# Rotating the last block's keys on GpSimd behind the second and third blocks' keys

## The reference

```python
x = x + mamba(layernorm(x))                      # in_proj, conv of 4 taps, selective scan over 16 states, out_proj
x = x + cross_attention(layernorm(x), ctx, pos, mask)
x = x + mixture(layernorm(x))                    # 64 experts of rank 8, the best 16 by a router

# cross attention: 32 heads of q, 8 heads of k and v (each serves 4 heads of q), head size 128
q = rows(query @ Wq);  k = rows(ctx @ Wk);  v = rows(ctx @ Wv)
cos, sin = tables[position_ids]
q = q * cos + rotate_half(q) * sin
k = k * cos + rotate_half(k) * sin               # rotate_half swaps the halves of the 128 and negates one
scores = q @ k.T / sqrt(128), masked with -1e9;  softmax;  @ v;  @ Wo
```

## Time and profile before

| | us |
|---|---|
| median of 3 runs | 2348.61 |
| lowest and highest | 2341.81, 2349.77 |
| the profiled execution's own time | 2350.73 |
| its span | 2349.1 |
| TensorE busy | 2086.0 (89%) |
| VectorE busy | 1762.5 (75%) |
| ScalarE busy | 1003.9 (43%) |
| GpSimd busy | 701.3 (30%) |
| seam behind stage 1, behind stage 2 | about 890 to 1000, about 1430 to 1540 |
| last stage | from about 2010 |

### The profile page before, as it was taken

How to read it: one execution, slowest core, us unless ns; L and a number is a source line. 1 busy time by engine, 2 the same in 40 slices (tenths; PEclk the granted TensorE clock), 3 DMA queues, 4 the chain that set the end, 5 groups by cost and what they waited for, 6 DMA issues and landing times.

```text
span 2349.1 us, 26708 instructions
## 1 busy us (share of the span) xinstructions
PE 2086.0 (89%) x8268; PEld 1192.0 (51%) x8272; DVE 1762.5 (75%) x1735; ACT 1003.9 (43%) x2549; POOL 701.3 (30%) x492
## 2 busy tenths in 40 slices
PE   6877887898999988998999989998999989799988
PEld 2333454345555543445556544345556544477774
DVE  4499994459999996259999996259999994456553
ACT  2544440265555532155545541255545540233331
POOL 0289992401111112401111111501111110456550
PEclk9788999889999999989999999989999999799999
DMA  2579895527888873435888874525887874332210
GB/s 63 165 178 230 210 215 169 146 95 175 176 182 196 184 180 101 154 117 135 186 190 179 186 166 119 186 91 136 190 190 181 188 166 117 103 99 90 86 59 18
DMA packets 117810, 352.12 MB, mean 150 GB/s; under 512 B 14016, under 2 KB 14144, under 8 KB 115296
## 3 DMA queue, kind: packets, MB, share of 16 engines
q0 software_dynamic: 40704, 146.82, 32.3%
q1 hardware_dynamic: 70112, 191.68, 26.6%
q10 hardware_dynamic: 6912, 12.59, 1.4%
HBM read 197.68 MB, written 23.33 MB: 94 GB/s over the span
## 4 chain that ended last, share of the span: by engine, by line
DVE 34%; PE 27%; DMA 17%; issue 14%; ACT 3%; POOL 2%; DVEq 1%; PEldq 1%; SPq 0%; POOLq 0%; PEld 0%; ACTq 0%
DMA xc<-hs 15%; DVE hs L1254 11%; DVE hs L1431 4%; PE acc L1753 4%; PE acc L1631 3%; DVE hs L1261 3%; DVE hs L1245 2%; PE pq L1684 2%; PE acc L1837 2%; PE pq L1714 2%; PE pq L1921 2%; PE pk L1921 2%; PE acc L1766 1%; DVE pzsc L1311 1%; DVE qr L1291 1%
## 5 line engine op out<-in xcount | busy, mean ns | idle before, releaser
L768 POOL DMA_DIRECT2D xc<-hs x192 | 164.1, 860 | 1116.3 <-DVE hs L1261 1095.9
L1254 DVE TENSOR_TENSOR_SCAN hs<-dA,hs 128x1024 f32<-128x1024 f32 x192 | 428.7, 2274 | 0.0
L988 ACT ACTIVATE dA<-dt,aneg 128x504 f32<-128x504 f32 x384 | 253.6, 707 | 320.0 <-DVE hs L1254 319.8
L1684 PE MATMUL pq<-qT,wa 128*128 128x512 f32 x768 | 354.1, 615 | 15.1 <-DVE pzsc L1311 14.9
L1766 PE MATMUL acc<-wb,oT 128*128 128x512 f32 x768 | 352.2, 603 | 3.6 <-ACT oT L976 3.6
L1261 DVE TENSOR_TENSOR hs<-hs,bc 128x1024 f32<-128x1024 f32 x256 | 307.6, 1203 | 2.2
L953 ACT ACTIVATE pr<-pzsc,mx 128x64 f32<-128x64 f32 x512 | 170.8, 335 | 245.1 <-DVE mx L1317 245.1
L1245 DVE TENSOR_TENSOR hs<-u,bc 128x1024 f32<-128x1024 f32 x192 | 227.5, 1217 | 26.6 <-DMA xc<-hs 21.0
L1631 PE MATMUL acc<-xnT,wa 128*128 128x512 f32 x512 | 234.4, 612 | 14.3 <-DMA wa<-in_wx 3.9
L1684 PEld LDWEIGHTS pq<-qT,wa 128*128 128x128 f32 x768 | 146.4, 196 | 189.3 <-issue 177.2
L1766 PEld LDWEIGHTS acc<-wb,oT 128*128 128x128 f32 x768 | 141.2, 193 | 148.0 <-issue 143.9
(11 more groups left out here) (255 smaller groups left out, 3379.2 us busy)
## 6 DMA issues: line engine op xcount, KB each, us to landing
xc<-hs POOLq DMA_DIRECT2D x240, 512.0 KB, 7.0
bc<-bc_rows SPq DMA_DIRECT2D x64, 512.0 KB, 7.5
wa<-in_wq SPq DMA_DIRECT2D x64, 512.0 KB, 10.2
wb<-in_wo SPq DMA_DIRECT2D x64, 512.0 KB, 7.0
wa<-in_wx SPq DMA_DIRECT2D x16, 512.0 KB, 7.0
wa<-in_wz SPq DMA_DIRECT2D x16, 512.0 KB, 3.8
wb<-in_ow SPq DMA_DIRECT2D x16, 512.0 KB, 6.3
wv<-in_wv SPq DMA_DIRECT2D x26, 256.0 KB, 13.1
```

What stands on the lines that cost most here:

```text
L768: G.dma_start(xc[:, 2 * c:2 * c + 2, :], hs[:, c, :].rearrange("p (d t) -> p d t", t=T), accum_op=ALU.add).then_inc(s_y[c], 16)
L988: ins = S.activation(to[:, :, 1:SEQ], dt[:, s, :].rearrange("p (b t) -> p b t", t=SEQ)[:, :, 1:SEQ], ACT.Exp, scale=aneg[:, s, bass.ds(jj ...
L1254: V.tensor_tensor_scan(out=hs[:, c, :], data0=dA[:, c % 2, :], data1=hs[:, c, :], initial=0.0, op0=ALU.mult, op1=ALU.add).then_inc(scd.sem, 1)
L1684: ins = M.matmul(pq[:, h, :], wa4(p)[:, k, h * P:(h + 1) * P], qT[:, k, :], start=(k == 0), stop=(k == KE - 1))
```

## The change

Block 3's eight heads are rotated by GpSimd as well, and the last stage loads them rotated. The seam behind stage 1 gets pairs 4 and 5 (heads 0 to 3 of block 3), the seam behind stage 2 the same for heads 4 to 7. Their tables are loaded by SyncE into `oT`. `rope_k` and its semaphores go. The slot waits are counted anew: three uses of each slot in a seam with six pairs.

```diff
-                eng.dma_start(to[:, :], src[b, g]).then_inc(s_k1, 16)      # load_k, load_raw_k
+                def load_turned_k(b, g, halves=True):
+                    eng.dma_start(kT[:, :], turned[b, g]).then_inc(s_k1, 16)
+                    for h in range(2 if halves else 0):
...
-                            if p == 0 and mamba:
+                            if p == 0:
                                 eng.wait_ge(sd.sem, sd.upto(blk, 1) + jj * 2)
                                 hold(eng)
-                                load_turned_k(blk, jj + 1)
-                            elif p == 0:
-                                eng.wait_ge(krdy.sem, krdy.upto(0, 0) + jj)
-                                hold(eng)
-                                load_raw_k(blk, jj + 1)
+                                load_turned_k(blk, jj + 1, mamba)
...
                     if not nxt:
-                        load_raw_k(i, 0)
+                        eng.wait_ge(sd.sem, sd.upto(blk, PAIRS - 1))
+                        load_turned_k(i, 0, False)
...
+                if attn and nxt:
+                    eng.wait_ge(wod.sem, wod.upto(blk, PAIRS - 1))
+                    for c in range(2):
+                        eng.dma_start(oT[:, c, :], tscr[NBLK - 1, c]).then_inc(s_cs3, 16)
...
-                        eng.wait_ge(s_kst[n], i * 32 + 32)
+                        eng.wait_ge(s_kst[n], i * 48 + 32)
...
                 def turn_pair(m, count):
+                    cos, sin = (cosT[:, :], sinT[:, :]) if m < pairs else (oT[:, 0, :], oT[:, 1, :])
...
-                    for m in range(KVH // 2):
-                        turn_pair(m)
+                    count = pairs + (2 if attn else 0)
+                    for m in range(count):
+                        if m == pairs:
+                            eng.wait_ge(s_cs3, i * 32)
+                        turn_pair(m, count)
...
                     if mamba:                                              # ScalarE, prefill
-                        eng.wait_ge(s_kst[1], blk * 32 + 32)
+                        eng.wait_ge(s_kst[1], i * 48 - 16)
...
+                if mamba and attn:                                         # VectorE, ahead of rope_q(0, 0)
+                    for n in range(2):
+                        eng.wait_ge(s_kst[n], i * 48 - 16)
...
-                    if not mamba and not tail and p == 0:
-                        rope_k(jj + 1)
...
-                        eng.wait_ge(krdy.sem, krdy.upto(0, o // 2) + jj)   # TensorE, scores of the last stage
+                        eng.wait_ge(s_k1, blk * (16 * KVH) + (o // 2 + 1) * 16 + jj * 16)
```

More of the change, by code:

```diff
@@ L97, in build @@
         vscr = nc.dram_tensor("v_rows", (KVH, P, T), F32, kind="Internal").ap()
-        turned = nc.dram_tensor("k_turned_rows", (NBLK - 1, KVH, P, T), F32, kind="Internal").ap()
+        turned = nc.dram_tensor("k_turned_rows", (NBLK, KVH, P, T), F32, kind="Internal").ap()
         tscr = nc.dram_tensor("rotary_rows", (NBLK, 2, P, T), F32, kind="Internal").ap()
@@ L171, in build @@
             "p (t e) -> p t e", e=EXPERTS)
[L173 to L177, removed]
+        rq = kr[0:RD, :]
+        gex = k1[:, 0:TT * EXPERTS].rearrange("p (t e) -> p t e", e=EXPERTS)
         def tab(b, t):
@@ L325, in build @@
         s_pid = sem("pos_index_ready")
-        kc1 = stage("pool_k_times_cos", KVH // 2)
-        kc2 = stage("pool_k_times_sin", KVH // 2)
-        kcd = stage("pool_k_turned", KVH // 2)
+        kc1 = stage("pool_k_times_cos", 6)
+        kc2 = stage("pool_k_times_sin", 6)
+        kcd = stage("pool_k_turned", 6)
         otd = stage("tail_o_done", TT)
@@ L339, in build @@
         q2r = stage("q_sin_ready", PAIRS)
-        krdy = stage("k_ready", KVH)
         vrdy = stage("v_ready", KVH)
@@ L536, in one @@
                 z_uses = W_DT if mamba else 0
-                def load_k(b, g, src, to, swapped):
-                    eng.dma_start(to[:, :], src[b, g]).then_inc(s_k1, 16)
-                    for h in range(2):
-                        eng.dma_start(swapped[h * 64:(h + 1) * 64, :], src[b, g, (1 - h) * 64:(2 - h) * 64, :]).then_inc(
+                def load_turned_k(b, g, halves=True):
+                    eng.dma_start(kT[:, :], turned[b, g]).then_inc(s_k1, 16)
+                    for h in range(2 if halves else 0):
+                        eng.dma_start(k2T[h * 64:(h + 1) * 64, :], turned[b, g, (1 - h) * 64:(2 - h) * 64, :]).then_inc(
                             s_kr, 16)
[L545 to L549, removed]
                 def load_tables(b):
@@ L837, in one, with heads_of, turns, slot_use @@
                         rstd(i, ln2, ln2r, TT)
+                pairs = KVH // 2
+                def heads_of(rows, m):
+                    if m < pairs:
+                        return rows[i, 2 * m:2 * m + 2]
+                    return rows[NBLK - 1, bass.ds((i - 1) * (KVH // 2) + 2 * (m - pairs), 2)]
+                def turns(m):
+                    return (i * 6 - 2 if attn else 0) + (m + 1 + LEAD)
+                def slot_use(m):
+                    return (i * 3 - 1 if attn else 0) + m // 2
                 def load_pair(m):
@@ L859, in turn_pair @@
                         load_pair(m + 1)
-                    eng.wait_ge(kc1.sem, kc1.upto(i, m))
+                    eng.wait_ge(kc1.sem, turns(m))
                     hold(eng)
-                    eng.wait_ge(kc2.sem, kc2.upto(i, m))
+                    eng.wait_ge(kc2.sem, turns(m))
                     hold(eng)
                     G.tensor_tensor(raw, raw, swp, ALU.subtract).then_inc(kcd.sem, 1)
-                    eng.wait_ge(kcd.sem, kcd.upto(i, m))
+                    eng.wait_ge(kcd.sem, turns(m))
@@ L866, in turn_pair @@
                     hold(eng)
-                    G.dma_start(turned[i, 2 * m:2 * m + 2].rearrange("g p t -> p g t"), raw).then_inc(s_kst[m % 2], 16)
+                    G.dma_start(heads_of(turned, m).rearrange("g p t -> p g t"), raw).then_inc(s_kst[m % 2], 16)
                 if nxt:
@@ L1326, in probs @@
                                     ALU.mult).then_inc(prdy.sem, 1)
-                return rope_q, rope_k, mask_scores, max_scores, invert_sum, probs
+                return rope_q, mask_scores, max_scores, invert_sum, probs
             norm_in(0)
@@ L1340, in one @@
                 blk = i - 1
-                rope_q, rope_k, mask_scores, max_scores, invert_sum, probs = attention_of(blk, mamba)
+                rope_q, mask_scores, max_scores, invert_sum, probs = attention_of(blk, mamba)
                 if not mamba:
@@ L1359, in one @@
                     eng.wait_ge(s_cs, blk * 32 + 32)
-                    if not mamba:
-                        rope_k(0)
                     rope_q(0, 0)
```

47 lines of the change are left out of this document (21 added, 26 removed).

## The result

The change makes the kernel slower: 2365.18 us, median of 4 runs (2362.48 to 2367.24), against 2345.58 us for the kernel before beside them (4 runs, 2341.81 to 2349.77). The ratio is 1.0082, 95% interval 1.0058 to 1.0107: about +20 us, where +28.5 was forecast. The profiled execution of after took 2363.53 us, its span is 2362.0 us.

What follows compares the result with a forecast made beforehand. Bound: a gapless chain of waits through TensorE, whose v and q wait for ScalarE's square behind the prefill. Seams +27.5, clock +6, last stage -5 make +28.5 us on 2348.61: 2377.1 us, range 2364 to 2394.

Steps and rivals of the forecast that it cites:

- The seams, +15.2 and +12.3: Two more pairs per seam delay prefill and square: +15.2 us behind stage 2, +12.3 behind stage 1, together +27.5.
- The period: Time each added pair takes in a seam: products 4.65, load issues 1.95, wait for loads 4.7, together 11.3 us.
- L: Time from the last load issue to the next pair's first product in a seam: taken as 4.7 us, bounds 3.8 and 6.9.
- rival 1: In the seams the new loads are as slow as the old, L 6.9: seams +36, time 2386 us, chance 0.15.
- TensorE's clock, +6: After idling in each seam, TensorE runs v and q at lower clock: 3 us per seam, bounds 0 and 5.
- What goes at no price: VectorE's new wait, SyncE's wait for the stores with what stands behind it, and the two table loads cost nothing.
- The last stage, -5: Taking rope_k out gains 7.8 us, late load and moved splits cost 2.8: -5, bounds -8 and 0.
- A step can give back 1.3 us and not 4.9: In the last stage, six steps with a head of k each save 1.3 us of TensorE's wait: -7.8.
- It fits by 0.5 us: In the last stage GpSimd's late splits end at 2164.9, before TensorE needs the second at 2165.4.
- the 2.8 taken off: Price in the last stage of the late wo load and of splits moving under VectorE's rotation of q: 2.8 us.
- rival 2's second way: In the last stage GpSimd's splits hold VectorE in six rotations of q, 1.95 us each: +11.7, 2389 us; chance 0.13 for both ways.
- Rival 3: The seams' two added pairs are hidden, only the last stage's gain of 7.8 us shows: 2341 us, chance 0.04.

Runs made afterwards that it cites:

- e4: The change with ScalarE's prefill moved behind the square, the root, v and dt in stages 1 to 3: 2340.81 us, ratio 0.999 to the kernel before.
- e3: The kernel before with the last stage's edit alone: four pairs per seam, no rotation of block 3's k: 2339.83 us, ratio 0.998.
- e7: The change with the last stage's load of the next k issued from ScalarE's queue instead of SyncE's: 2357.43 us, ratio 1.0062 to the kernel before.
- e9: The change with late prefill, output store ahead of SyncE's wait for pairs, and wo's odd half loaded before its wait for scores: 2319.12 us, ratio 0.9889.
- e2: The kernel before with the seams' edit alone: six pairs on GpSimd, last stage still rotating k on VectorE: 2371.07 us, ratio 1.0113.

## Why the prediction was right, and where it was off

- **The bound and the mechanism: right.** The chain runs through the square, the prefill stands in front of it, and the last pair's store releases the prefill. Moving the prefill back (e4) takes 22 to 24 us away, some 5 of them behind stage 0, where the prediction didn't look: there the prefill already held the square in the kernel before.
- **The seams, +15.2 and +12.3: right.** From the x projection to the grouped mean it was +15.7 and +13.9. The period was put at 11.3 and is 11.4, with L near the 4.7 of the first pair, and not 6.9: rival 1 is out. The Trainium skill's estimate (page "DMA: Bandwidth & Descriptors", section "Anatomy of one DMA — SWDGE (gpsimd) path") would have L at its floor of 3.8. From the end of the last issue to the product, L is 1519.51 - 1514.44 = 5.1 us for the fifth pair and 1530.90 - 1526.04 = 4.9 for the sixth, so the trace doesn't agree.
- **TensorE's clock, +6: right in size (5.2, and 3 to 6 over all traces), off in shape.** I had the clock back 10 us after work began; in the two seams it was back after 4 to 5. It fell while TensorE was still idle, so most of the low stretch cost nothing.
- **What goes at no price: one step failed unseen.** "Behind SyncE's stand three loads, the output store and the B and C rows, which need the root": I had weighed the rows of B and C and passed over the output store, whose landing ScalarE's `dt` waits for. In the change the root is so late that this cost nothing, but it was next in line, 6.8 us in e4.
- **The last stage, -5: right as a sum (-5 to -7 in the trace, -4 in e3's median), but by luck, out of two wrong terms.** "A step can give back 1.3 us and not 4.9" was too little: with the loads in order, GpSimd's splits of `wo` come every 30.0 to 30.3 us per pair of steps (e7, e9) instead of 31.3 to 33.4, 32.5 on average, in the kernel before (31.7 in after). So the stage is 15 to 18 us shorter than the old one, not 8. "It fits by 0.5 us" and the 2.8 taken off for the late `wo` load and the moved splits was too little as well: it is 10 us between after and e7. I had named the splits' move under VectorE's rotation of q and given it no price of its own. Ten of the 16 multiplies, all from 2125 to 2269, take 1.9 to 3.5 us instead of 1.22, 11.9 us more in all. That is rival 2's second way. That its price of 11.7 is met is chance, since it was six rotations at 1.95; only the other term was so much larger that the stage gained all the same. "It fits by 0.5 us" held for the splits themselves: TensorE waited for none of them. These are its waits from 2060 to 2270 in after (total, times, longest), and both are for VectorE:

```profile
PE pk L1726 <- DVE oT_lo L1381: 8.6, 11, 1.7
PE pq L1715 <- DVE qp L1280: 8.5, 7, 5.4
```

- **The size, 28.5 against about 20.** The terms, read in the traces, add up to 29.6 + 5.2 - 5 to -7, that is 28 to 30. The medians say 20 (e2 alone: 27.5 where its seams show 33 to 34). Outside the terms the code is the same and the traces scatter by 2 to 8 us a stretch, and after was the quicker there. One stretch may be more than scatter: from the clearing of the accumulators behind stage 1 to the next x projection it is 432.0, 434.3 and 433.4 us in the three kernels whose square is held in these seams (after, e2, e7), and 433.9 to 438.1 in the nine others. Whether and how a delay shortens what follows, no run here settles, so the missing 8 to 10 us stay open.
- **Rival 3: its condition, that the prefill could go without the pairs, doesn't hold in the change.** Where it was made to hold, in e4, it gave 2340.81. The 2341 worked out for it is met by chance: against the kernel before beside it that is -2.8 and not -7.8, and in it are two late output stores and a gain behind stage 0, neither of which the prediction had.

## What to carry to other kernels

An idle engine is no free engine: ask which instruction waits for its last result, and what stands behind that instruction in its stream, then move the waiting one rather than the work. When one wait is taken away, look for the next one behind it before judging the idea; here a change that lost 20 us became a gain of 26 by moving three instructions (the prefill, the output store and one load). Ask also whether such a move would help without the change: about a quarter of this gain lies in a place that the change leaves as it was. A load whose condition comes later holds back every load behind it on its queue, so when a source or a wait changes, re-sort the queue by when each transfer can start.

## What the runs showed of the hardware

- **A TENSOR_TENSOR of GpSimd holds a multiply of VectorE's until it ends.** Timelines of the last stage, kernel after; VectorE, then GpSimd:

```profile
2125.10 3.45 DVE L1277 TENSOR_TENSOR qr<-qr,sinT 128x1024 f32<-128x1024 f32 x1
...
2157.58 2.71 DVE L1277 TENSOR_TENSOR qr<-qr,sinT 128x1024 f32<-128x1024 f32 x1
...
2173.79 2.00 DVE L1277 TENSOR_TENSOR qr<-qr,sinT 128x1024 f32<-128x1024 f32 x1
```

```profile
2125.08 2.40 POOL L726 TENSOR_TENSOR wq_lo<-wa,wq_hi 128x1024 fp32r<-128x1024 f32 x1
...
2156.80 2.41 POOL L726 TENSOR_TENSOR wq_lo<-wa,wq_hi 128x1024 fp32r<-128x1024 f32 x1
...
2173.67 2.77 POOL L724 TENSOR_SCALAR wq_hi<-wa 128x1024 fp32r<-128x1024 f32 x1 [0.37 <-POOL wo_lo L726]
```

  Both long multiplies end 1.1 us after GpSimd's TENSOR_TENSOR (2127.48 to 2128.55, and 2159.21 to 2160.29), close to their own 1.22 us: they seem to make little or no headway beside it. This agrees with the Trainium skill, page "SBUF — State Buffer", section "SBUF: two separate sides", whose rule is an exclusive lock on a shared port pair, the loser blocked. The third, beside GpSimd's TENSOR_SCALAR, takes 2.00 us instead of 1.22 and ends at 2175.79, before that instruction does at 2176.44. So it isn't held for the whole of it, and here the trace doesn't agree with the rule. The multiply by the cosine just ahead (L1276), which reads q where TensorE wrote it (`pq`), takes 1.22 or 1.23 us in all 16 steps, also at 2156.44, where GpSimd's TENSOR_TENSOR of 2156.80 runs beside it.
- **The clock falls in the middle of an idle stretch.** In both seams of after it fell 2 to 4 us into the idle time and was low for 17 us, of which 4 to 5 lay after work had begun again, where the last stage of before took some 10.
- **The loads of GpSimd's queue were slower the busier the DMA engines were.** In after, behind stage 2, the wait in front of a pair's first product was 4.19 us for the third pair (DMA share 1.00 from 1490 to 1496), 1.88 for the fourth (0.87 from 1500 to 1508), and 1.24 and 1.06 for the last two (0.71 from 1512 to 1520, 0.69 from 1524 to 1531), when SyncE issued no loads. No run varied the traffic alone.
